# Attention value products: one block per sequence in every second period instead of two half blocks, with eight probability buffers instead of four

## The chip, the cores and the metric

The kernel runs on one NeuronCore of a Trainium2 chip. The metric is the device time of one execution in microseconds (us). Engines are named as the profile names them: PE (TensorE, matmuls), PEld (its weight loads), DVE (VectorE), ACT (ScalarE), POOL (GpSimd), SP (the queue that issues most DMAs).

## What is computed

A decoder of two layers over 32 sequences of 128 tokens with 256 channels, all in float32. Each layer is: layer norm, self-attention, residual; layer norm, attention over a context, residual; layer norm, feed-forward, residual. Three of the six parts are multi-head attentions with 16 heads of 16 channels, and the change lies in these three. Cut to what matters:

```python
def mha(xq, xkv):                      # self-attention: xq is xkv
    q, k, v = split_heads(xq @ Wq), split_heads(xkv @ Wk), split_heads(xkv @ Wv)
    scores = einsum('bhqd,bhkd->bhqk', q, k) / sqrt(16)
    probs = softmax(scores)            # over 128 keys
    out = einsum('bhqk,bhkd->bhqd', probs, v)
    return merge_heads(out) @ Wo
```

The first one (stage a0 below) also has rotary position factors on q and k and biases; the third (stage a2) takes k and v from the context and has a key mask and biases.

## The kernel before, in words

The six parts are six stages, one after the other: a0 (self-attention, about 15 to 285 us of the profile), b0, c0, a1 (self-attention, about 680 to 935 us), a2 (masked attention over the context, about 935 to 1240 us), d1. Stages a0, a1 and a2 are three calls of one function, `attention_stage` (line 526).

**Tiling.** A stage works on 16 groups (NG) of two sequences (PAIR). A group has 8 steps (STEPS): steps 0 to 3 belong to its first sequence, steps 4 to 7 to its second, and a step is four heads of one sequence (QH). Per step and engine:

- `scores` (PE, lines 952 and 961) computes the scores twice, in two banks of PSUM: S1 (queries on the rows, one pass) for the row maxima, S2 (keys on the rows, three passes with split high and low parts) for the exponent. It uses row strips of 32: an S matmul contracts over 32 rows only, and the matmuls of two steps alternate. In stage a2 `mask_step` (line 993) adds the mask to S1.
- `max_step` (DVE, line 830) takes the row maxima of S1. In stage a2 a `shift_step` of POOL (line 687) forms mask minus maximum from it.
- `shift_step` (PE, line 1006, or 1003 in stage a2) subtracts the maxima in S2. PE does this one pair of steps after `scores`.
- `exp_step` (ACT, line 723) writes exp of S2 into a buffer of `probs`, one of four. It waits until the value products of the step that used the buffer before are done (`av_full`).
- `av_step` (PE, line 1019) multiplies probabilities by values: four matmuls per step, one per head, each with 32 columns of weights (16 value channels and a column of ones for the denominator), so the four heads lie in four column strips of the array. Output is bank AV[0] for the first sequence, AV[1] for the second. Each of these float32 matmuls is two records in the trace.

After the four steps of a sequence ACT copies its AV bank out (`raw_heads`, line 728), PE turns it (`turn`, line 1026), DVE divides by the denominators (lines 836 and 839), PE turns it back (`turn_back`, line 1032), ACT and DVE split it into high and low parts (lines 733 and 843).

**Order.** Every engine has its own program, and the order in each is written out by hand. For PE it is `group` at the end of the function: four periods per group, t = 0, 2, 4, 6, each handling two steps. A period of PE is, in this order: `scores` of steps t and t+1 (and the three passes of steps t-2 and t-1), in a2 the mask, `shift_step` of t-2 and t-1, `turn` (t = 0 and 4) or `turn_back` (t = 2 and 6), then one piece of projection work: at t = 0 `output` of an earlier group and `transposes` of the next group's normalised input (line 188), at t = 2 `queries` of the next group, at t = 4 its `keys`, at t = 6 its `values` (all on line 104). The period ends with `av_step` of steps t-4 and t-3, 8 matmuls. Steps with a negative number belong to the group before.

**Waits around it.** PE executes in program order. `scores` of a period waits for the row maxima of the steps before (`max_ok`) and for the exps of the pair whose S2 banks it writes again (`exp_ok`). `queries` waits for the low part of the transposed input, which DVE makes (line 198) from what ACT has copied (line 194) from the output of `transposes`. In stage a2, POOL's program at t = 4 is: shift of step 4, the layer norm's reciprocal root of a later group (`pool_rstd`, lines 172 and 174), shift of step 5; PE needs both shifts at t = 6.

Of the kernel before, what the change touches and what calls it, by code (L numbers as in the profile page):

```python
# [18 lines left out]
ACT = mybir.ActivationFunctionType  # L19
AXX = mybir.AxisListType.X  # L20

P = 128
# [6 lines left out]
H, DH = 16, 16  # L29
QH = 4  # L30
HV = 2
NQ = H // QH
STEPS = PAIR * NQ
# [11 lines left out]
def at_least(eng, sem, value):  # L45

    if not isinstance(value, int) or value > 0:
        eng.wait_ge(sem, value)
# [19 lines left out]
class Names:  # L68
# [7 lines left out]
    def sb(self, name, shape, dt=FP32):  # L76
        return self.ctx.enter_context(self.nc.sbuf_tensor(f"{self.stage}_{name}", shape, dt))
# [4 lines left out]
    def sem(self, name):  # L82
        handle = self.sem_ctx.enter_context(self.nc.semaphore(f"{self.stage}_{name}"))
        self.sems.append(handle)
        return handle
# [440 lines left out]
def attention_stage(nc, name, before, norm, next_norm, consts, wt, following, spare, context=None, next_context=None, mask_dram=None,  # L526
# [3 lines left out]
    sb, sem = nm.sb, nm.sem  # L530
    ident, ident_b, neg_ident_b, head_mask = (consts[k] for k in ("ident", "ident_b", "neg_ident_b", "head_mask"))

    probs = sb("probs", [P, 4, QH * P])
    if x_dram is not None:
        wt.stage(nm, probs[:, 0:KC, :])
    following.stage(nm)
# [23 lines left out]
    S2 = [nm.ps(f"S2_{i}") for i in range(2)]  # L560
# [26 lines left out]
    s1_full, max_ok, s2_full, exp_ok, av_full = (sem(n) for n in ("s1_full", "max_ok", "s2_full", "exp_ok", "av_full"))  # L587
# [22 lines left out]
    def has_window(G):  # L610
        return not isinstance(G, int) or G + 1 < NG
# [9 lines left out]
    def has_step(G, t):  # L621

        return not isinstance(G, int) or 0 <= STEPS * G + t < STEPS * NG

    def whole(G):
        return not isinstance(G, int) or 0 <= G < NG

    def place(t, parity):

        tt = t % STEPS  # L630
        return tt // NQ, tt % NQ, (1 - parity if t < 0 else parity)
# [13 lines left out]
    with nc.Block() as block:  # L645
# [70 lines left out]
        def _(act):  # L716
            if x_dram is None:
                wt.wait_in(act)
            def exp_step(G, t, parity):
                T = G * STEPS + t  # L720
                act.wait_ge(s2_full, T + 1)
                at_least(act, av_full, T - 3)
                act.activation(probs[:, t % 4, :], S2[t % 2][:], ACT.Exp, scale=DH ** -0.5).then_inc(exp_ok, 1)  # L723

            def raw_heads(B, b):
                act.wait_ge(av_full, B * NQ + NQ)
# [219 lines left out]
        def _(pe):  # L946
# [18 lines left out]
            def scores(G, t, parity):  # L965

                T = G * STEPS + t
                first, second = has_step(G, t), has_step(G, t - 2)
                if cross and isinstance(G, int) and G == 0 and t == 0:
                    pe.wait_ge(setup, 1)  # L970
                if first:
                    if t == 0:
                        pe.wait_ge(qmhi_ok, HV * (G + 1))
                        pe.wait_ge(khi_ok, G + 1)
                    at_least(pe, max_ok, T)
                if second:
                    if t == 2:
                        pe.wait_ge(qmlo_ok, HV * (G + 1))
                        pe.wait_ge(klo_ok, G + 1)
                    at_least(pe, exp_ok, T - 2)  # L980
                for i in range(3 * KC):
                    if second:
                        for u in range(2):
                            s2_pass(t - 2 + u, parity, i // 3, i % 3)
                    if first and i < KC * HV:
                        for u in range(2):
                            last = s1_head(t + u, parity, i // HV, i % HV)
                            if i == KC * HV - 1 and not cross:
                                last.then_inc(s1_full, 1)

            def mask_step(G, t):

                pe.matmul(S1[t % 2][:], ident_b[:], add_mask[:].rearrange("p h k -> p (h k)"), start=False, stop=True,  # L993
                          skip_group_check=True).then_inc(s1_full, 1)
# [15 lines left out]
            def av_step(G, t, parity):  # L1010
                T = G * STEPS + t
                b, j, par = place(t, parity)
                if t == 0:
                    pe.wait_ge(v_free, G + 1)
                if t % NQ == 0:
                    at_least(pe, olo_ok, G * PAIR + t // NQ - 1)
                pe.wait_ge(exp_ok, T + 1)
                for h in range(QH):
                    last = pe.matmul(AV[b][32 * h:32 * h + 32, j * P:(j + 1) * P], v_pad[par][:, b, j * QH + h, :],  # L1019
                                     probs[:, t % 4, h * P:(h + 1) * P], start=True, stop=True)  # L1020
                last.then_inc(av_full, 1)

            def turn(B, b):
                pe.wait_ge(raw_ok, B + 1)
                for r in range(NQ):
                    last = pe.transpose(AV[b][:, r * P:(r + 1) * P], av_raw[:, r * P:(r + 1) * P], ident[:])
                last.then_inc(turned, 1)
# [93 lines left out]
            def group(G, parity):  # L1121
                for t in range(0, STEPS, 2):
                    if vo_bias and t == 0 and isinstance(G, int) and G == 0:
                        pe.wait_ge(vo_added, PAIR)
                    scores(G, t, parity)
                    if cross and has_step(G, t):
                        mask_step(G, t)
                        mask_step(G, t + 1)
                    if has_step(G, t - 2):
                        shift_step(G, t - 2)  # L1130
                        shift_step(G, t - 1)
                    if t in (0, 4) and whole(G - 1):
                        turn((G - 1) * PAIR + t // 4, t // 4)
                    if t in (2, 6) and whole(G - 1):
                        turn_back((G - 1) * PAIR + t // 4, t // 4)
                    if t == 0 and whole(G - 2):
                        output(G - 2)
                    if t == 0:
                        transposes(G)
                    if t == 2 and has_window(G):  # L1140
                        queries(G, parity)
                    if t == 4 and has_window(G):
                        keys(G)
                    if t == 6 and has_window(G):
                        values(G)
                    if vo_bias and t == 6 and isinstance(G, int) and G < 0:
                        value_bias()
                    if t == 6 and isinstance(G, int) and G == NG:
                        output(G - 1)
                    if has_step(G, t - 4):  # L1150
                        av_step(G, t - 4, parity)
                        av_step(G, t - 3, parity)
                    if isinstance(G, int) and G >= NG - 1:
                        for u in range(2):
                            following.pe_slot(pe, (G - NG + 1) * STEPS + t + u, NEXT_BANKS,
                                              ((next_norm.lo_ok, 1), (max_ok, NG * STEPS)))
# [819 lines left out]
```

## Time and profile before

| what | us |
|---|---|
| median of 3 runs (lowest, highest) | 1435.04 (1432.97, 1438.40) |
| the profiled execution's own time | 1437.27 |
| its span, first to last instruction | 1435.5 |
| PE busy in the span | 1344.6 (94%) |
| PEld busy | 1195.7 (83%) |
| DVE busy | 1002.7 (70%) |
| ACT busy | 781.9 (54%) |
| POOL busy | 371.4 (26%) |

Matmuls are pipelined: one record lasts some 0.27 us although the next starts 0.11 us after it, so times of PE are read from start to start. A row of the timeline gives the start (us from the span's start), the time to the end of the last record that it merges, the engine, the line, the operation, output <- inputs, partitions x elements, the number of records merged, and in brackets the idle time before it with the work that ended it. The order of the rows is that of their starts.

### The profile page before, as it was taken

To read this page: it belongs to the slowest core of one execution; us is meant where nothing else is said; L and a number is where in the kernel's file an instruction comes from. 1 tells how busy PE (TensorE), PEld (TensorE's weight loads), DVE (VectorE), ACT (ScalarE), POOL (GpSimd) and SP (SyncE) were. 2 spreads that over 40 slices of the span, in tenths; PEclk is the share of its full clock that TensorE was granted. 3 is DMA by queue.
4 is the path that set the end of the run, shared out by engine and by line. 5 is a ranking of instruction groups with operands and counts; after the bars stand their busy time and mean duration, and the time that the engine had idled before them with its cause. 6 is when DMAs were issued, how large, how long until landed. Compare 5 with 4: busy or idle time off the path is not lost. (4 is left out here: it accounts for less than half of the span.)

```text
span 1435.5 us, 41753 instructions
## 1 busy us (share of the span) xinstructions
PE 1344.6 (94%) x15796; PEld 1195.7 (83%) x15796; DVE 1002.7 (70%) x2423; ACT 781.9 (54%) x1569; POOL 371.4 (26%) x458
## 2 busy tenths in 40 slices
PE   5999999899978999998999999889999999689887
PEld 5888888789968999998888888778888888578777
DVE  5888888555555545454777777677777777688885
ACT  2555555345554445453655555545555556377786
POOL 1212212011011212110000000055555555134442
PEclk9999999999998999999999999999999999899999
DMA  6000000031000000001000000020000000000000
GB/s 226 3 2 0 0 0 2 2 117 37 29 21 10 1 0 0 0 1 44 10 3 0 0 0 1 2 78 20 17 15 15 15 8 2 1 16 22 29 23 30
DMA packets 16478, 28.74 MB, mean 20 GB/s; under 512 B 3616, under 2 KB 7712, under 8 KB 16000
## 3 DMA queue, kind: packets, MB, share of 16 engines
q1 hardware_dynamic: 16384, 27.44, 5.8%
q8 instruction: 64, 1.05, 0.3%
q14 instruction: 30, 0.25, 0.1%
HBM read 23.24 MB, written 4.19 MB: 19 GB/s over the span
## 5 line engine op out<-in xcount | busy, mean ns | idle before, releaser
L723 ACT ACTIVATE a_probs<-a_S 128x512 f32<-128x512 f32 x384 | 208.5, 594 | 155.3 <-PE a_S L1006 85.9
L830 DVE TENSOR_REDUCE a_row_max<-a_S 128x4 bf16<-128x512 f32 (+1 forms) x384 | 247.1, 685 | 54.9 <-PE a_S L993 33.1
L172 POOL TENSOR_TENSOR all_var_eps<-all_moments,all_ln_eps 128x2 f32<-128x2 f32 x96 | 25.0, 261 | 727.9 <-DVE all_moments L167 727.9
L961 PE MATMUL a_S<-a_qm_hi,all_odd_split 32*128 32x256 f32 x1536 | 188.7, 303 | 7.6 <-DVE a_row_max L830 3.6
L961 PEld LDWEIGHTS a_S<-a_qm_hi,all_odd_split 32*128 32x128 f32 x1536 | 132.0, 184 | 46.8 <-issue 39.0
L687 POOL TENSOR_TENSOR a_shifts<-a_add_mask,a_row_max 128x512 bf16<-128x512 bf16 x128 | 131.0, 1039 | 119.4 <-DVE a_row_max L830 119.4
L952 PE MATMUL a_S<-all_odd_split,a_qm_hi 32*128 32x128 f32 x1536 | 127.8, 284 | 1.7 <-DVE all_odd_weights L938 1.7
L1019 PE MATMUL a_AV<-a_probs,a_v_pad 128*32 128x128 f32 x3072 | 123.7, 279 | 0.0
L180 DVE TENSOR_SCALAR all_xn<-all_x_res,all_moments,all_rstd 128x256 f32 (+1 forms) x192 | 99.6, 560 | 19.6 <-POOL all_rstd L174 18.8
L961 PE MATMUL a_S<-a_qm_lo,all_odd_split 32*128 32x256 f32 x768 | 108.9, 277 | 0.0
L952 PEld LDWEIGHTS a_S<-all_odd_split,a_qm_hi 32*128 32x128 f32 x1536 | 100.6, 186 | 2.7 <-DVE all_odd_weights L938 2.5
L104 PE MATMUL c_OUT<-all_odd_split,c_h_hi 128*128 128x256 f32 x512 | 94.8, 283 | 0.9 <-DVE all_x_res L1574 0.9
L1019 PEld LDWEIGHTS a_AV<-a_probs,a_v_pad 128*32 128x32 f32 x3072 | 72.2, 109 | 27.5 <-issue 9.8
L843 DVE TENSOR_TENSOR all_odd_split<-a_AV,all_odd_split 128x256 fp32r<-128x256 f32 x96 | 40.8, 425 | 66.1 <-ACT all_odd_split L733 66.1
L104 PE MATMUL a_FA<-all_odd_split 128*128 128x256 f32 x576 | 84.2, 298 | 2.8 <-DVE all_odd_split L843 2.8
L1726 ACT ACTIVATE d_y<-d_ZT,all_even_weights 128x256 f32<-128x256 f32 x128 | 65.0, 559 | 33.4 <-PE d_ZT L1803 33.4
L104 PEld LDWEIGHTS c_OUT<-all_odd_split,c_h_hi 128*128 128x128 f32 x512 | 80.9, 192 | 1.0 <-issue 1.0
L728 ACT ACTIVATE a_av_raw<-a_AV 128x512 f32<-128x512 f32 x96 | 57.8, 602 | 42.9 <-PE a_AV L1019 42.7
L1503 ACT ACTIVATE c_h<-c_HB,all_odd_weights 128x256 f32<-128x256 f32 x128 | 53.8, 472 | 49.6 <-PE c_HB L1613 48.7
L1006 PE MATMUL a_S<-all_neg_ident_b,a_row_max 128*128 128x128 bf16 x1024 | 79.8, 221 | 0.0
L104 PEld LDWEIGHTS a_FA<-all_odd_split 128*128 128x128 f32 x576 | 75.2, 199 | 3.7 <-DVE all_odd_split L843 3.4
L174 POOL TENSOR_TENSOR all_rstd<-all_var_eps,all_minus_half 128x2 f32<-128x2 f32 x96 | 73.6, 767 | 7.5
(250 smaller groups left out, 3869.5 us busy)
## 6 DMA issues: line engine op xcount, KB each, us to landing
all_cx<-in_ctx SPq DMA_DIRECT2D x32, 256.0 KB, 2.7
all_x_res<-in_x SPq DMA_DIRECT2D x8, 512.0 KB, 8.0
out_x<-all_x_res SPq DMA_DIRECT2D x16, 256.0 KB, 2.0
b_routed_wi<-in_L_ffn_wi_W SPq DMA_DIRECT2D x1, 1024.0 KB, 5.2
b_routed_wo<-in_L_ffn_wo_W SPq DMA_DIRECT2D x1, 1024.0 KB, 7.1
all_even_weights<-in_L_ffn_W_fc SPq DMA_DIRECT2D x1, 1024.0 KB, 5.3
all_even_weights<-in_L_ffn_W_proj SPq DMA_DIRECT2D x1, 1024.0 KB, 7.0
a_a_raw<-in_L_attn_Wqkv SPq DMA_DIRECT2D x1, 512.0 KB, 4.0
```

The costliest lines, as they stand in the source:

```text
L104: last = pe.matmul(out, w(k), m(k), start=(k == 0 and n == 0), stop=(k == chunks - 1 and n == 2))
L174: pool.tensor_tensor(self.rstd[:], self.var_eps[:], self.minus_half[:], ALU.pow).then_inc(self.rstd_ok, 1)
L180: last = dve.tensor_scalar(self.xn[:, b, :], self.x(w, b), self.moments[:, b, 0:1], self.rstd[:, b:b + 1], ALU.subtract, ALU.mult)
L687: pool.tensor_tensor(shifts[:, t % 4], add_mask[:], row_max[:, t % 4, :].rearrange("p (h o) -> p h o", o=1).to_broadcast([P, QH, P]), ALU. ...
L723: act.activation(probs[:, t % 4, :], S2[t % 2][:], ACT.Exp, scale=DH ** -0.5).then_inc(exp_ok, 1)
L728: act.activation(av_raw[:], AV[b][:], ACT.Copy).then_inc(raw_ok, 1)
L830: dve.tensor_reduce(row_max[:, t % 4, :], S1[t % 2][:].rearrange("p (h k) -> p h k", h=QH), AXX, ALU.max).then_inc(max_ok, 1)
L952: return pe.matmul(S1[t % 2][:, at * P:(at + 1) * P], qm_hi[parity][strip, c, b, v, :], k_hi[parity][strip, c, tok], start=(not cross or a ...
L961: pe.matmul(S2[t % 2][:, c * HV * P:(c + 1) * HV * P], k[par][strip, c, tok], q[par][strip, c, b].rearrange("p h t -> p (h t)"), start=(c ...
L1006: last = pe.matmul(part, row_max[:, t % 4, h:h + 1].to_broadcast([P, P]), neg_ident_b[:], start=False, stop=h == QH - 1, skip_group_check= ...
L1019: last = pe.matmul(AV[b][32 * h:32 * h + 32, j * P:(j + 1) * P], v_pad[par][:, b, j * QH + h, :], probs[:, t % 4, h * P:(h + 1) * P], star ...
L1726: last = act.activation(y32[n][:, m * TOK:(m + 1) * TOK], ZT[n][:, m * TOK:(m + 1) * TOK], ACT.Identity, bias=offset[:, f:f + 1], scale=ga ...
```

## The change

It alters three things in `attention_stage`: `probs` has 8 buffers (STEPS) instead of 4, so that a step's number in the group is its buffer; `exp_step` waits for the value products of eight steps before instead of four; and PE no longer does two steps of value products at the end of each period, but four steps, all of one sequence, at the end of the periods t = 2 (steps 4 to 7 of the group before) and t = 6 (steps 0 to 3 of this group). The periods t = 0 and t = 4 have none.

```diff
-    probs = sb("probs", [P, 4, QH * P])
+    probs = sb("probs", [P, STEPS, QH * P])
...
-                at_least(act, av_full, T - 3)
-                act.activation(probs[:, t % 4, :], S2[t % 2][:], ACT.Exp, scale=DH ** -0.5).then_inc(exp_ok, 1)
+                at_least(act, av_full, T - STEPS + 1)
+                act.activation(probs[:, t % STEPS, :], S2[t % 2][:], ACT.Exp, scale=DH ** -0.5).then_inc(exp_ok, 1)
...
                 for h in range(QH):
                     last = pe.matmul(AV[b][32 * h:32 * h + 32, j * P:(j + 1) * P], v_pad[par][:, b, j * QH + h, :],
-                                     probs[:, t % 4, h * P:(h + 1) * P], start=True, stop=True)
+                                     probs[:, t % STEPS, h * P:(h + 1) * P], start=True, stop=True)
...
-                    if has_step(G, t - 4):
-                        av_step(G, t - 4, parity)
-                        av_step(G, t - 3, parity)
+                    if t in (2, 6) and has_step(G, t - 6):
+                        for u in range(NQ):
+                            av_step(G, t - 6 + u, parity)
```

The order of PE's instructions in stage a0, group 1, at the end of its period t = 4 (`keys` into bank FB, then the scores of the next period):

```order
 L104 MATMUL a_FB<-all_xT_hi,all_odd_split 128x256 x2
 L104 MATMUL a_FB<-all_xT_lo,all_odd_split 128x256
-L1019 MATMUL a_AV<-a_probs,a_v_pad 32x128 x8
 L961 MATMUL a_S_0<-a_qm_hi,all_odd_split 128x256
 L961 MATMUL a_S_1<-a_qm_hi,all_odd_split 128x256
```

The block of 8 value products is gone, and the scores follow the keys directly. The same holds at the end of t = 0, where the transposes stand ahead of it.

The order of PE at the end of the period t = 6 of the same group (`values` into bank FA, then the scores of the next group):

```order
 L104 MATMUL a_FA<-all_odd_split,all_xT_lo 128x256
 L104 MATMUL a_FA<-all_odd_split,all_xT_hi 128x256
-L1019 MATMUL a_AV<-a_probs,a_v_pad 32x128 x8
+L1019 MATMUL a_AV<-a_probs,a_v_pad 32x128 x16
 L961 MATMUL a_S_0<-a_qm_hi,all_odd_split 128x256
 L961 MATMUL a_S_1<-a_qm_hi,all_odd_split 128x256
```

The block has grown to 16. The same holds at the end of t = 2, behind the queries. The orders of DVE and of POOL are unchanged.

The order of ACT in the loop of stage a0, with the semaphores waited for (`exp_step` between its other work):

```order
 L739 ACTIVATE a_qm_hi<-a_q,all_head_mask 128x4x128
 L721 REGISTER_ALU
-L723 ACTIVATE a_probs<-a_S_0 128x512 [waits a0_av_full,a0_s2_full]
-L721 REGISTER_ALU
-L723 ACTIVATE a_probs<-a_S_1 128x512 [waits a0_av_full,a0_s2_full]
+L48 REGISTER_ALU [waits a0_s2_full]
+L723 ACTIVATE a_probs<-a_S_0 128x512 [waits a0_av_full]
+L721 REGISTER_ALU
+L48 REGISTER_ALU [waits a0_s2_full]
+L723 ACTIVATE a_probs<-a_S_1 128x512 [waits a0_av_full]
```

The exps stay where they were; the value waited for needs one more register instruction ahead of each, which now carries the wait for the scores.

## Rows read from the trace of the kernel before

**Rows 1.** Page, part 1: busy us (share of the span) and instructions

```profile
PE 1344.6 (94%) x15796; PEld 1195.7 (83%) x15796; DVE 1002.7 (70%) x2423; ACT 781.9 (54%) x1569; POOL 371.4 (26%) x458
```

**Rows 2.** Windows over the steady parts of a0, a1, a2: length, then busy us

```profile
core 0: us, PE busy (x) PEld busy (x) DVE busy (x) ACT busy (x) POOL busy (x), PEclk, DMA share, GB/s
57.00:275.00 218.00, 216.93 (x3336) 189.65 (x3332) 181.52 (x391) 119.12 (x234) 42.05 (x52) 1.00 0.00 1
700.00:925.00 225.00, 222.94 (x3443) 194.44 (x3442) 173.51 (x370) 129.95 (x248) 12.17 (x27) 1.00 0.00 1
960.00:1215.00 255.00, 254.28 (x3626) 213.01 (x3625) 194.13 (x427) 142.29 (x275) 151.24 (x158) 1.00 0.05 13
```

**Rows 3.** Page, part 5: the value products, all stages

```profile
L1019 PE MATMUL a_AV<-a_probs,a_v_pad 128*32 128x128 f32 x3072 | 123.7, 279 | 0.0
```

**Rows 4.** Timeline of PE, a1 group 0: queries to scores directly, then keys, block, scores

```profile
685.43 0.28 PE L104 MATMUL a_FA<-all_xT_lo,all_even_split 128*128 128x256 f32 x1
685.64 0.39 PE L961 MATMUL a_S<-a_qm_hi,all_odd_split 32*128 32x256 f32 x2
...
688.36 0.28 PE L104 MATMUL a_FB<-all_xT_lo,all_even_split 128*128 128x256 f32 x1
688.57 0.64 PE L1019 MATMUL a_AV<-a_probs,a_v_pad 128*32 128x128 f32 x16
689.14 0.39 PE L961 MATMUL a_S<-a_qm_hi,all_odd_split 32*128 32x256 f32 x2
```

**Rows 5.** Windows of 0.01 us inside that block: (x) is its records in flight

```profile
688.56:688.57 0.01, 0.00 (x1) 1.00 0.00 0
688.69:688.70 0.01, 0.01 (x4) 1.00 0.00 0
688.72:688.73 0.01, 0.01 (x8) 1.00 0.00 0
688.80:688.81 0.01, 0.01 (x8) 1.00 0.00 0
688.83:688.84 0.01, 0.01 (x12) 1.00 0.00 0
688.91:688.92 0.01, 0.01 (x8) 1.00 0.00 0
688.94:688.95 0.01, 0.01 (x12) 1.00 0.00 0
```

**Rows 6.** Timeline of a1: transposes at t = 0, their split, queries at t = 2

```profile
804.30 0.60 PE L188 MATMUL a_FB<-all_ident,all_xn 128*128 128x128 f32 x4
804.93 0.60 ACT L194 ACTIVATE all_xT_hi<-a_FB 128x512 fp32r<-128x512 f32 x1 [1.36 <-PE a_FB L188]
805.57 0.69 DVE L198 TENSOR_TENSOR all_xT_lo<-a_FB,all_xT_hi 128x512 fp32r<-128x512 f32 x1 [0.26 <-ACT all_xT_hi L194]
806.89 0.30 PEld L104 LDWEIGHTS a_FA<-all_xT_hi,all_even_split 128*128 128x128 f32 x2
```

**Rows 7.** Timeline of a0: the last exps of a group against the next scores

```profile
207.36 1.07 ACT L723 ACTIVATE a_probs<-a_S 128x512 f32<-128x512 f32 x2
208.68 0.39 PE L961 MATMUL a_S<-a_qm_hi,all_odd_split 32*128 32x256 f32 x2
```

**Rows 8.** Timeline of a2, periods t = 4 and 6: mask, maxima, POOL, shift products

```profile
1112.73 0.60 PE L993 MATMUL a_S<-a_add_mask,all_ident_b 128*128 128x512 bf16 x2
1113.40 1.29 DVE L830 TENSOR_REDUCE a_row_max<-a_S 128x4 f32<-128x512 f32 x2
1114.18 1.04 POOL L687 TENSOR_TENSOR a_shifts<-a_add_mask,a_row_max 128x512 bf16<-128x512 bf16 x1 [2.54 <-DVE a_row_max L830]
1115.45 1.16 POOL L174 TENSOR_TENSOR all_rstd<-all_var_eps,all_minus_half 128x2 f32<-128x2 f32 x1
1116.58 1.03 POOL L687 TENSOR_TENSOR a_shifts<-a_add_mask,a_row_max 128x512 bf16<-128x512 bf16 x1
1117.07 0.60 PE L993 MATMUL a_S<-a_add_mask,all_ident_b 128*128 128x512 bf16 x2
1117.50 1.29 DVE L830 TENSOR_REDUCE a_row_max<-a_S 128x4 f32<-128x512 f32 x2 [0.79 <-PE a_S L993]
1117.52 0.61 PE L1003 MATMUL a_S<-all_ident_b,a_shifts 128*128 128x128 bf16 x8
```

**Rows 9.** Timeline of a2, group 0: PE waits for POOL between two shift products

```profile
958.91 0.40 PE L1003 MATMUL a_S<-all_ident_b,a_shifts 128*128 128x128 bf16 x4 [0.92 <-POOL a_shifts L687]
```

**Rows 10.** Timeline of PE and ACT at the end of stage a1

```profile
918.50 0.39 PE L961 MATMUL a_S<-a_qm_hi,all_odd_split 32*128 32x256 f32 x2 [0.98 <-DVE a_row_max L830]
...
928.07 0.64 PE L1019 MATMUL a_AV<-a_probs,a_v_pad 128*32 128x128 f32 x16
928.78 0.60 ACT L728 ACTIVATE a_av_raw<-a_AV 128x512 f32<-128x512 f32 x1 [0.22 <-PE a_AV L1019]
```

## The prediction

> **What bounds the kernel now.** I read the page first: PE is busy 94% of the span [rows 1]. That is an average over six stages, so I took the steady part of each attention stage by itself: PE is busy 216.93 of 218 us in a0, 222.94 of 225 in a1 and 254.28 of 255 in a2, at a granted clock of 1.00, while DVE, the next, has 181.52, 173.51 and 194.13 [rows 2]. So in these stages PE's own stream sets the time: what shortens it counts fully, as long as no other engine becomes late. Then I read the timeline around the value products, from start to start, to see what a block of them costs on PE, and last, for each wait that PE passes, how long before PE's arrival the work was done.
>
> **What a block costs.** The change computes nothing less: 3072 records of value products in 192 blocks of 16 records [rows 3] become 96 blocks of 32. What can be saved is what a block costs beside its own streaming. Group 0 of a1 shows the pair side by side. Without a block, the last projection matmul and the first scores matmul start 0.21 us apart (685.43, 685.64). With one, the block starts 0.21 us behind the projection, and the scores 0.57 us behind the block (688.57, 689.14) [rows 4]. So a block of 8 matmuls costs 0.57 us. Inside it the records start in waves of four, one per column strip: 688.565, then near 688.70, 688.81 and 688.92, that is 0.135, 0.11 and 0.11 us apart, and the exit from the last wave to the scores is 0.22 us, 0.11 more than one more wave would take [rows 5, 4]. Eight more matmuls in a block that is already running are four more waves, 4 x 0.11 = 0.44 us. **Each removed block therefore saves 0.57 - 0.44 = 0.13 to 0.135 us**: one exit (0.11) and a slow first wave (0.025). The bounds: nothing, if every further step in a long block costs what it costs in a block of its own; 0.17 us, if a wave takes 0.10 us, which windows of 0.01 us leave open. I take 0.135, since three of the four intervals are direct readings.
>
> The Trainium skill, "TensorEngine Tiling (Array Packing)", Key Properties, says that changing the tiling mode, and not merely the tile, drains the engine. The trace agrees that a change of shape costs time: 0.21 us from projection to scores against 0.11 between like matmuls. By the rule alone a removed block would save one such change, 0.10 us, 8.9 us for 89 blocks where the rows give 12.0.
>
> **How many.** Each attention stage loses 32 blocks, 96 in all. They count only where PE is the bound. At the end of a1 and a2 the engine waits for row maxima that DVE, busy with the next stage's weights, delivers late (0.98 us in one case) [rows 10]; there the three blocks of the last group and the drain save nothing. I give a0 31, a1 29 and a2 29: 89 x 0.135 = **-12.0 us**.
>
> **What PE meets earlier.** In a group the period ends t = 0 and t = 4 come 0.57 us sooner, and t = 2 and t = 6 come 0.44 later. Behind each there is a wait.
>
> - t = 0 to t = 2, **queries** wait for the split of the transposes: they end at 804.90, ACT copies until 805.53, DVE is done at 806.26, and PE loads the first weights at 806.89 [rows 6]. That is 0.63 us of slack, of which 0.57 goes. A release takes 0.03 to 0.04 us in these rows (804.90 to 804.93, 805.53 to 805.57); I take 0.05 for PE. It just fits: 0 to 0.1 us per group, and I take 0. In a2 the mask and the context transposes add time ahead of it.
> - t = 6 to t = 0, **scores** wait for the exps of steps 4 and 5: done at 208.43, needed at 208.68 [rows 7]. These exps hang on a chain through DVE that starts at the queries of t = 2; between that and the scores PE's stream becomes longer (+0.44 - 0.57 + 0.44 = +0.31), so the slack grows. The extra register instruction ahead of each exp lies on ACT, which is busy 119 of 218 us [rows 2], and inside this slack. Cost 0; without the slack it would be a few hundredths of a us per exp.
> - t = 4 to t = 6 in **a2**, the shift products wait for POOL. POOL starts the shift of step 4 0.78 us behind the start of the maxima, then the reciprocal root (1.16 us), then the shift of step 5, done at 1117.61, which is 3.43 us after POOL's start. PE's products with it are the fifth to eighth of the eight records that start at 1117.52, 0.056 us apart, so they start at 1117.74 [rows 8]: a slack of 0.13 us less 0.05 for the release. With the change PE is there 0.44 - 0.57 = 0.13 us sooner, counted from the queries, at 1117.61. And POOL is later: the maxima of step 4 start at 1113.40 because DVE was busy until then, although the mask product started at 1112.73; the mask product of the new order starts 0.44 us later, at 1113.17, and maxima start 0.43 us behind it (1117.07, 1117.50) [rows 8], at 1113.60. So POOL ends 0.20 us later, at 1117.81, and PE goes on at 1117.86: **a new wait of 0.25 us**, in the 15 groups that have the reciprocal root, **+3.75 us**. Behind it on PE stand the turn back, the values and all that follows, so it counts. That this wait is real can be seen in group 0, where PE already stands 0.92 us for POOL at this place [rows 9]. Its bounds are 0 (POOL just in time) and 0.92 us.
>
> **The eight buffers** take away nothing that was waited for: no exp waits for value products in the rows of the steady parts. The bank AV is freed by work of t = 3 and t = 7, and its first write only comes later than before.
>
> **Ends of the stages.** In the drain, ACT copies the bank as soon as the last value product is done [rows 10]; that block now has 16 matmuls, +0.44 us, and PE has 0.57 us less ahead of it, some of it then spent in waiting. Between -0.4 and +1.3 us for three stages; I take +0.4.
>
> **Sum:** -12.0 + 3.75 + 0.4 = -7.85 us. Against the profiled execution, 1437.27, that is 1429.4; against the median of the runs, 1435.04, which is 2.2 us lower, it is **1427.2 us**. A measurement of this kernel can tell about 0.5%, 7.2 us, from no change; the forecast is just past that, at 0.55%.
>
> **Rivals.**
>
> 1. *POOL stays in time in a2*, and all 89 blocks count: -12.0 + 0.4 gives 1423.4. For it: spans of POOL are rough, and its end leads PE's need by only hundredths. Against: both the delayed maxima and the earlier PE point the same way. Chance 0.2.
> 2. *The saving is eaten almost everywhere*: the queries of a0 and a1 wait 0.1 us (30 groups, 3 us), and a wave in a long block takes 0.12 (89 x 0.04 = 3.6 us), which leaves -7.85 + 6.6 = -1.3, 1433.8. For it: 0.63 us of slack against 0.62 needed. Against: no row of a stall there. Chance 0.22.
> 3. *Slower*: POOL's wait has the size of group 0, 0.92 us in 15 groups of a2, 13.8 us instead of 3.75, with the drain at its bad end (+1.3): -12.0 + 13.8 + 1.3 = +3.1, 1438.1. With the drain as I took it, the change loses from (12.0 - 0.4) / 15 = 0.77 us per such group on. For it: the place is the same; against: in group 0 POOL started later for reasons of the start. To be slower by more than 0.5% a wait of (12.0 + 7.2) / 48 = 0.40 us would have to appear in every group of all three stages. Chance 0.08, 0.05 of it past 0.5%.
>
> My forecast itself has a chance of 0.5. It is so near the bound of 0.5% that I count 0.3 of it as faster and 0.2 as within. **Faster by over 0.5%:** 0.3 + 0.19 of rival 1 = 0.49. **Within 0.5%:** 0.2 + 0.01 + 0.22 + 0.03 = 0.46. **Slower:** 0.05. The range goes from rival 1 less 1 us for a shorter wave (1422.5) to rival 2 (1434).
>
> **What the profile would show.** Blocks of 32 records that take 1.01 us from their start to the scores' (0.97 to 1.05 fits); 0.21 us from projection or transposes to scores at the ends of t = 0 and t = 4. A group of a0 and of a1 shorter by 0.27 us, a group of a2 by 0.02 (the period of two groups of a0 by 0.54 us). In a2 a stall of about 0.25 us between the fourth and the fifth product on line 1003, put down to POOL, fifteen times, and no stall of PE on line 104 in a0 and a1. The forecast is wrong if the block takes over 1.1 us, if groups of a2 shrink as those of a1 do, or if the scores wait for exps or maxima in the steady part.

## The result, and the profile after

| | before | changed |
|---|---|---|
| median of 6 runs (lowest, highest), us | 1436.62 (1432.97, 1438.64) | 1423.38 (1420.69, 1427.06) |
| the profiled execution's own time | 1437.27 | 1422.83 |
| its span | 1435.5 | 1420.9 |

The ratio is 0.9912, with an interval of 0.9897 to 0.9927: the changed kernel is faster by 0.9%, which is more than the 0.5% that a measurement can tell. The time lies inside the range that was given. The gain, 13.2 us by the medians, is larger than the forecast 7.85. The same kernel timed again beside other runs of before gave 1426.26 against 1435.66, 0.9936 (0.9923 to 0.9949), 9.4 us. Between such comparisons the median of one kernel moves by up to 3 us, so I count on a gain of 9 to 13 us.

The page of the changed kernel, part 1, with busy us, share of the span and instructions, against [rows 1]; and the row of the value products from part 5, against [rows 3]:

```profile
PE 1329.2 (94%) x15796; PEld 1197.8 (84%) x15796; DVE 1001.7 (70%) x2423; ACT 782.4 (55%) x1569; POOL 371.4 (26%) x458
...
L1019 PE MATMUL a_AV<-a_probs,a_v_pad 128*32 128x128 f32 x3072 | 103.8, 276 | 0.0
```

Nothing less is computed: 15796 matmul records and 3072 of value products, as before. PE's busy time fell by 15.4 us, about as much as the span. The value products' busy time counts each stretch in which at least one record is in flight, and it fell from 123.7 to 103.8 although a record takes as long as before (276 ns, 279 before): the tail of a block, in which its last records are still in flight, is there 96 times and no longer 192.

**The block.** Timeline of PE in the changed kernel, a1 group 0, where [rows 4] are from: keys directly followed by scores, then values, block, scores.

```profile
682.50 0.28 PE L104 MATMUL a_FB<-all_xT_lo,all_even_split 128*128 128x256 f32 x1
682.71 0.38 PE L961 MATMUL a_S<-a_qm_hi,all_odd_split 32*128 32x256 f32 x2
...
685.44 0.28 PE L104 MATMUL a_FA<-all_even_split,all_xT_hi 128*128 128x256 f32 x1
685.65 1.08 PE L1019 MATMUL a_AV<-a_probs,a_v_pad 128*32 128x128 f32 x32
686.66 0.38 PE L961 MATMUL a_S<-a_qm_hi,all_odd_split 32*128 32x256 f32 x2
```

The block of 32 records takes 1.01 us from its start to the scores' (685.65, 686.66), and keys to scores 0.21 us (682.50, 682.71), both as forecast. The second half of a block is indeed 0.44 us, not 0.57.

**The groups.** A period of a group is read from one block of transposes (line 188) to the next. Timeline of PE in before, stage a0, then in the changed kernel:

```profile
196.43 0.60 PE L188 MATMUL a_FB<-all_ident,all_xn 128*128 128x128 f32 x4
...
211.93 0.60 PE L188 MATMUL a_FB<-all_ident,all_xn 128*128 128x128 f32 x4
227.49 0.60 PE L188 MATMUL a_FB<-all_ident,all_xn 128*128 128x128 f32 x4
```

```profile
192.28 0.60 PE L188 MATMUL a_FB<-all_ident,all_xn 128*128 128x128 f32 x4
...
207.50 0.60 PE L188 MATMUL a_FB<-all_ident,all_xn 128*128 128x128 f32 x4
222.72 0.60 PE L188 MATMUL a_FB<-all_ident,all_xn 128*128 128x128 f32 x4
```

| period of a group, us | before | in before, at the end of a loop pass | changed | at the end of a loop pass |
|---|---|---|---|---|
| a0 | 15.50 | 15.75 | 15.22 | 15.24 to 15.29 |
| a1 | 15.62 | 15.84 to 15.87 | 15.34 | 15.38 to 15.42 |
| a2 | 17.74 | 17.95 to 18.06 | 17.74 | 17.77 to 17.81 |

The groups of a0 and a1 are shorter by 0.28 (forecast 0.27), those of a2 by nothing (forecast 0.02). But in before every second group inside the loop was some 0.23 us longer, and in the changed kernel it hardly is. The loop has five passes and so four branches back, and each stage has four such groups; behind the fifth pass, where PE goes straight on, there is none. That column I had not seen.

**The wait in a2.** Timeline of the changed kernel, the periods t = 4 and 6, where [rows 8] are from:

```profile
1101.19 0.60 PE L993 MATMUL a_S<-a_add_mask,all_ident_b 128*128 128x512 bf16 x2
1101.62 1.29 DVE L830 TENSOR_REDUCE a_row_max<-a_S 128x4 f32<-128x512 f32 x2
1102.39 1.04 POOL L687 TENSOR_TENSOR a_shifts<-a_add_mask,a_row_max 128x512 bf16<-128x512 bf16 x1 [2.73 <-DVE a_row_max L830]
1103.66 1.16 POOL L174 TENSOR_TENSOR all_rstd<-all_var_eps,all_minus_half 128x2 f32<-128x2 f32 x1
1104.79 1.03 POOL L687 TENSOR_TENSOR a_shifts<-a_add_mask,a_row_max 128x512 bf16<-128x512 bf16 x1
1105.40 0.88 PE L1003 MATMUL a_S<-all_ident_b,a_shifts 128*128 128x128 bf16 x8
1105.88 0.23 PEld L1003 LDWEIGHTS a_S<-all_ident_b,a_shifts 128*128 128x128 bf16 x4 [0.27 <-POOL a_shifts L687]
```

The mask product is 0.43 us ahead of the maxima, POOL ends at 1105.82, and the fifth shift product is loaded at 1105.88. The eight products take 0.88 us instead of 0.61: a wait of 0.27 us where 0.25 was forecast. It doesn't stand on PE's row, since the matmuls are pipelined; the row of the weight load has it, in each of the groups 1 to 14. In group 0 the wait of [rows 9], which PE's row does show, grew from 0.92 to 1.24 us.

**Where the 14.6 us of the two spans lie:** from the transposes in group 1 to the last ones in group 15, 14 periods, a0 gives 4.66 us, a1 4.35 and a2 0.58, together 9.6. The other 5.0 us lie outside these stretches: 0.67 ahead of a0's, 0.67 from a0's to a1's, 0.62 from a1's to a2's, and 3.05 behind a2's. So three readings needed tests: the block and the wait, the loop's end, and what lies outside the stretches.

### The profile page after: what moved, and what is told of

The parts are those of the page before. It is cut to its first block and busy times, and to the rows that moved or that the text cites. A ratio compares the mean times of both kernels' runs of the same rounds, so it can differ in the third digit from the quotient of the medians.

```text
span 1420.9 us, 41741 instructions
## 1 busy us (share of the span) xinstructions
PE 1329.2 (94%) x15796; PEld 1197.8 (84%) x15796; DVE 1001.7 (70%) x2423; ACT 782.4 (55%) x1569; POOL 371.4 (26%) x458
## 5 line engine op out<-in xcount | busy, mean ns | idle before, releaser
L1019 PE MATMUL a_AV<-a_probs,a_v_pad 128*32 128x128 f32 x3072 | 103.8, 276 | 0.0
L1019 PEld LDWEIGHTS a_AV<-a_probs,a_v_pad 128*32 128x32 f32 x3072 | 78.0, 109 | 13.0 <-issue 1.5
```

## Experiments

The theory: a removed block gives 0.14 us, a2 gives most of it back to POOL, and the ends of loop passes give what I had overlooked. The rivals: the buffers or the exps do it (an earlier exp frees the S2 banks); or a wait of PE's other than the loop's was removed.

**1. The buffers alone.** The first three hunks of the change, PE's order as before.

```diff
-    probs = sb("probs", [P, 4, QH * P])
+    probs = sb("probs", [P, STEPS, QH * P])
...
-                at_least(act, av_full, T - 3)
+                at_least(act, av_full, T - STEPS + 1)
```

> Eight probability buffers and the looser wait of the exps, with the value products still in two steps per period. My theory: the buffers free nothing that was waited for, so the time is that of the kernel before, within 1.5 us, and the groups of a0 keep their 15.50 and 15.75 us. Rival (the buffers themselves bring a part of the 13 us measured): 3 us or more faster.

Measured: 1434.88 beside 1436.02 of before, ratio 0.999 (0.998 to 1.0), and every period of the table as in before. Eight buffers by themselves give nothing that can be told from no change.

**2 and 3. One merge at a time.** Eight buffers; in the first kernel only the first sequence's products are done together (t = 6), in the second only the second's (t = 2).

```diff
-                    if has_step(G, t - 4):
+                    if t == 6 and has_step(G, 0):
+                        for u in range(NQ):
+                            av_step(G, u, parity)
+                    if t in (0, 2) and has_step(G, t - 4):
                         av_step(G, t - 4, parity)
                         av_step(G, t - 3, parity)
```

```diff
-                    if has_step(G, t - 4):
+                    if t == 2 and has_step(G, -4):
+                        for u in range(NQ):
+                            av_step(G, u - 4, parity)
+                    if t in (4, 6) and has_step(G, t - 4):
                         av_step(G, t - 4, parity)
                         av_step(G, t - 3, parity)
```

> Eight buffers; only the first sequence of a group is merged: a block of 16 at the end of t = 6, none at t = 4, blocks of 8 at t = 0 and t = 2 as before. Block theory: 46 counting blocks x 0.135 = 6.2 us faster. Loop theory (the 0.22 us stall at the loop's end, 15 times, goes where the block ahead of the branch has 16 matmuls): 3.3 us more. POOL theory: PE reaches the shift products of a2 0.57 us earlier against a slack of 0.08, so it waits 0.49 us in 15 groups: 7.4 us back. Sum: about 2 us faster than before, a group of a2 0.36 us longer than the 17.74 of before. Without the POOL theory: 9.5 us faster.

> Eight buffers; only the second sequence is merged: a block of 16 at the end of t = 2, none at t = 0, blocks of 8 at t = 4 and t = 6. Block theory: 6.2 us faster. Loop theory: the block ahead of the branch is still one of 8, so the 0.22 us stall stays. POOL theory: PE reaches the shift products later, no wait, a group of a2 is 17.60 us. Sum: 6 us faster than before. If the loop's stall goes here too, 9.5 us.

Measured: the merge at t = 6 gives 1436.12, ratio 1.0001 (0.9991 to 1.0012), nothing where some 2 us were expected; the merge at t = 2 gives 1428.66, 0.9954 (0.9941 to 0.9967), 7.4 us where 6 were. The periods tell why. With t = 6 merged, a group of a0 takes 15.40 (15.48 at the loop's end) and of a1 15.48, so 0.10 to 0.14 less each, and the long groups at the loop's end are gone but for 0.03 to 0.09 us; but a group of a2 takes 18.00 outside the loop and 18.11 to 18.15 in it, 0.26 to 0.41 more than 17.74. Timeline of this kernel in a2:

```profile
1113.70 1.16 POOL L174 TENSOR_TENSOR all_rstd<-all_var_eps,all_minus_half 128x2 f32<-128x2 f32 x1
...
1115.19 0.39 PE L1003 MATMUL a_S<-all_ident_b,a_shifts 128*128 128x128 bf16 x4
...
1115.92 0.23 PEld L1003 LDWEIGHTS a_S<-all_ident_b,a_shifts 128*128 128x128 bf16 x4 [0.52 <-POOL a_shifts L687]
1115.92 0.40 PE L1003 MATMUL a_S<-all_ident_b,a_shifts 128*128 128x128 bf16 x4 [0.35 <-POOL a_shifts L687]
```

The wait for POOL is 0.52 us here: the period t = 4 has lost its whole block, so PE is 0.57 us sooner, and nothing was added ahead of it at t = 2. First and fifth product are 0.73 us apart where 0.22 would do ([rows 8]: eight products start 0.056 us apart), and this 0.51 less the 0.14 of a removed block is the 0.37 by which the groups in the loop are longer. Outside the loop PE's row shows a wait of 0.23 instead of 0.35, and the group is 0.26 longer. With t = 2 merged, POOL isn't waited for (the block at t = 4 is still there), a2 takes 17.60, 0.14 less, a0 15.36, 0.14 less, and the long groups stay (15.6 in a0, 15.69 in a1, 17.83 in a2). So a removed block is worth 0.14 us in each stage, the wait comes from t = 4, and what happens at the loop's end comes from the block at t = 6.

**4 and 5. Without the loop.** The 16 groups of a stage written out instead of a loop of two groups, for before and for the changed kernel.

```diff
-        for G in range(-1, 3):
-            group(G, G % 2)
-        with eng.Fori(1, (NG - 4) // 2) as i:
-            group(i * 2 + 1, 1)
-            group(i * 2 + 2, 0)
-        for G in range(NG - 3, NG + 1):
+        for G in range(-1, NG + 1):
             group(G, G % 2)
```

> The kernel before with all groups of the attention stages written out, no loop on any engine. Loop theory: 15 stalls of 0.22 us go, 3.3 us faster, all groups of a0 take 15.50 us. Rival (the longer groups have another cause, such as the parity of the group): no change and alternating groups.

> The changed kernel with no loop in the attention stages. Loop theory: the stall at the loop's end is already gone, so within 1 us of the changed kernel, 13 us faster than before. Against the unrolled kernel before it shows the blocks and the POOL wait alone: 8 to 10 us.

Measured: before without the loop 1433.77, ratio 0.9987 (0.9976 to 0.9997), 2.25 us less (2.8 by the rows of the three stretches), and the groups that ended a pass lose their extra 0.2 us (15.50 in a0 with some of 15.56, 15.62, 17.74). The changed kernel without the loop takes 1422.3, 0.9912 (0.9896 to 0.9929), and its profiled execution has the periods that it has outside the loop; the three stretches are 0.7 us shorter. So before lost 2.8 us at the loop's end, and the changed kernel loses 0.7. The lines in before, at the end of a pass in a2, first PE's timeline, then the weight loads':

```profile
1101.75 0.64 PE L1019 MATMUL a_AV<-a_probs,a_v_pad 128*32 128x128 f32 x16
1102.55 0.39 PE L961 MATMUL a_S<-a_qm_hi,all_odd_split 32*128 32x256 f32 x2 [0.15 <-issue]
```

```profile
1102.54 0.19 PEld L961 LDWEIGHTS a_S<-a_qm_hi,all_odd_split 32*128 32x128 f32 x2 [0.42 <-issue]
```

The block takes 0.80 us to the scores, not the 0.57 of [rows 4], and no engine is named as the one waited for: "issue". PE's branch back to the loop's start stands between the two. The same place in the changed kernel:

```profile
1090.09 1.08 PE L1019 MATMUL a_AV<-a_probs,a_v_pad 128*32 128x128 f32 x32
1091.13 0.39 PE L961 MATMUL a_S<-a_qm_hi,all_odd_split 32*128 32x256 f32 x2
```

```profile
1091.12 0.19 PEld L961 LDWEIGHTS a_S<-a_qm_hi,all_odd_split 32*128 32x128 f32 x2 [0.22 <-issue]
```

That is 1.04 us instead of the 1.01 elsewhere. The weight load still stands, 0.22 us instead of 0.42, but behind a block of 1 us little of it reaches the matmuls: the stall is hidden and not gone. Between the two kernels without a loop the medians differ by 11.5 us, where 8 to 10 were expected (the two stood beside different runs of before), and the spans of their profiles by 11.1. Of it the stretch of a0 gives 4.0, that of a1 3.7 and that of a2 -0.2, 7.5 in all, a little less than 28 x 0.28 = 7.8 because PE waits for an exp in group 1 of each stage of the changed kernel (0.16 us on its row). 3.6 us by the spans are left for what lies outside.

**6 and 7. POOL's reciprocal root after both shifts.** In POOL's program the root moves from t = 4 to t = 5, behind the shift of step 5; once on the changed kernel, once on before.

```diff
-                    if has_norm(G) and t == 4:
+                    if has_norm(G) and t == 5:
                         norm.pool_rstd(pool, G + 2)
-                    if first_of_next(G) and t == 4:
+                    if first_of_next(G) and t == 5:
                         next_norm.pool_rstd(pool, 0)
```

> The changed kernel with POOL's reciprocal root moved behind the shift of step 5 instead of ahead of it. POOL theory: the wait of 0.27 us between the shift products of a2 goes in 15 groups, a group of a2 falls from 17.74 to 17.47 us, 4 us faster than the changed kernel, about 17 us faster than before. Rival (PE is held by something else there, or the normalisation becomes late by the later root): no gain, or up to 1 us per group lost in a wait for the transposes.

> The kernel before with the same move on POOL alone. Theory: the wait did not exist before the change (PE had 0.08 us of slack), so the time is that of the kernel before within 1.5 us. Rival (the wait was there before): up to 4 us faster.

Measured on the changed kernel: 1420.25 against 1435.57, 0.99 (0.9882 to 0.9917), 15.3 us where about 17 were expected. The period of a2 is 17.47 instead of 17.74, 0.27 less, while a0 and a1 stay, and group 0 of a2 is 1.35 us shorter. Timeline of a2:

```profile
1099.04 2.04 POOL L687 TENSOR_TENSOR a_shifts<-a_add_mask,a_row_max 128x512 bf16<-128x512 bf16 x2 [2.73 <-DVE a_row_max L830]
1101.03 0.64 POOL L172 TENSOR_TENSOR all_var_eps<-all_moments,all_ln_eps 128x2 f32<-128x2 f32 x1
1101.76 1.09 POOL L174 TENSOR_TENSOR all_rstd<-all_var_eps,all_minus_half 128x2 f32<-128x2 f32 x1
...
1102.04 0.61 PE L1003 MATMUL a_S<-all_ident_b,a_shifts 128*128 128x128 bf16 x8
```

Both shifts are done 0.96 us before the products, which take 0.61 us again. On before the same edit gives 1433.39, 0.9988 (0.9973 to 1.0002), and leaves the steady periods at 17.74 and 17.95; only group 0, with the wait of [rows 9], is shorter by 1.1 us. So before had no wait in the steady part, the changed kernel has one of 0.27 us per group, and its cause is the root between the two shifts.

**8. The changed order with four buffers.** PE's order of the change, `probs` with four buffers and the old wait.

```diff
-    probs = sb("probs", [P, STEPS, QH * P])
+    probs = sb("probs", [P, 4, QH * P])
...
-                at_least(act, av_full, T - STEPS + 1)
+                at_least(act, av_full, T - 3)
```

> The new order of the value products with the old four buffers and the old wait of the exps. Theory: the exps of steps 4 and 5 (and 0 and 1) can start only when the block has done its first steps, some 0.5 us into it, and take 1.09 us, so the scores behind the block wait about 0.6 us, twice per group, 94 times: 60 us slower than the changed kernel. Rival (the buffers are not needed): as the changed kernel.

Measured: 1524.65, ratio 1.062 (1.0597 to 1.0644), 101 us over the changed kernel where I expected some 60. Periods 17.23, 16.75 and 20.78. Timeline of a0:

```profile
165.37 1.08 PE L1019 MATMUL a_AV<-a_probs,a_v_pad 128*32 128x128 f32 x32
165.86 1.08 ACT L723 ACTIVATE a_probs<-a_S 128x512 f32<-128x512 f32 x2 [2.89 <-PE a_AV L1019]
167.09 0.39 PE L961 MATMUL a_S<-a_qm_hi,all_odd_split 32*128 32x256 f32 x2 [0.64 <-ACT a_probs L723]
170.95 0.39 PE L961 MATMUL a_S<-a_qm_hi,all_odd_split 32*128 32x256 f32 x2 [0.51 <-ACT a_probs L723]
174.05 1.08 PE L1019 MATMUL a_AV<-a_probs,a_v_pad 128*32 128x128 f32 x32
175.74 0.39 PE L961 MATMUL a_S<-a_qm_hi,all_odd_split 32*128 32x256 f32 x2 [0.61 <-ACT a_probs L723]
```

ACT stands 2.89 us for the block, its exps are late, and PE stands for them: block to scores is 1.72 and 1.69 us instead of 1.01. Those two waits, 0.68 to 0.71 us per block, were expected; the third (0.51 us, behind the period without a block) was not: ACT's late exps push back its other work and, through it, DVE's, which feeds ACT again. The three, 0.71, 0.68 and 0.51, are 1.9 of the 2.0 us by which a group of a0 is longer; the 3.0 us in a2 I did not take apart. So the buffers give nothing by themselves, and without them the new order costs more than it brings.

**9. The blocks cut in two.** In the changed kernel 8 of the 16 matmuls of a block are done ahead of the period's projection, so there are 192 blocks again, in other places.

```diff
+                    if t in (2, 6) and has_step(G, t - 6):
+                        for u in range(2):
+                            av_step(G, t - 6 + u, parity)
                     if t == 2 and has_window(G):
                         queries(G, parity)
...
                     if t in (2, 6) and has_step(G, t - 6):
-                        for u in range(NQ):
+                        for u in range(2, NQ):
```

> The changed kernel with each block of 16 cut in two: 8 value products ahead of the queries (t = 2) or the values (t = 6), 8 behind them. Block theory: every cut adds a change of shape on the way in (0.21 - 0.11 = 0.10 us), a slow first wave (0.025) and an exit (0.11): 0.235 us, 0.47 per group, about 90 times, 21 us slower than the changed kernel. Rival (only the number of changes between value products and scores counts): as the changed kernel.

Measured: 1456.89, ratio 1.0151 (1.0138 to 1.0164), 30.6 us more than the changed kernel beside it (1426.26), where I expected 21. Periods: 15.91 in a0, 16.00 in a1, 18.36 to 18.41 in a2, so 0.62 to 0.69 more per group, and 0.22 more at the loop's end, since the block ahead of the branch is short again. Timeline of a0, period t = 2:

```profile
209.94 0.39 PE L1032 MATMUL a_AV<-all_ident,a_o_tok 128*128 128x128 f32 x2
210.25 0.64 PE L1019 MATMUL a_AV<-a_probs,a_v_pad 128*32 128x128 f32 x16
210.83 0.39 PE L104 MATMUL a_FA<-all_odd_split,all_xT_hi 128*128 128x256 f32 x1
211.05 0.28 PE L104 MATMUL a_FA<-all_odd_split,all_xT_lo 128*128 128x256 f32 x1
...
212.44 0.65 PE L1019 MATMUL a_AV<-a_probs,a_v_pad 128*32 128x128 f32 x16
213.01 0.39 PE L961 MATMUL a_S<-a_qm_hi,all_odd_split 32*128 32x256 f32 x2
```

A block costs more here than between projection and scores. Turn back to projection takes 0.15 us without a block between them and 0.89 with it (209.94 to 210.83), and the projection itself starts as slowly with the block as without (0.22 us between its first two matmuls here, 0.20 in a1 of the changed kernel, at 684.05, where no block stands ahead). The second block takes 0.57. A cut thus costs 0.89 - 0.15 + 0.57 - 1.01 = 0.30 us in these rows and 0.31 to 0.35 by the periods: that a block costs something beside its streaming is shown a second time, and that the amount depends on its neighbours too.

**10. The products ahead of the values.** At t = 6 the whole block stands ahead of `values` instead of behind them.

```diff
+                    if t == 6 and has_step(G, 0):
+                        for u in range(NQ):
+                            av_step(G, u, parity)
                     if t == 6 and has_window(G):
                         values(G)
...
-                    if t in (2, 6) and has_step(G, t - 6):
+                    if t == 2 and has_step(G, t - 6):
```

> The changed kernel with the block of t = 6 ahead of the values, so that the values stand between it and the scores. One more change of shape per group, 0.10 us: 4.6 us slower than the changed kernel. It also tests what goes ahead of the loop's branch: 24 records of projection that run for 1.5 us instead of 64 of value products that run for 1.0. If the stall at the loop's end is hidden by running time ahead of the branch, it stays away; if it needs the long block there, it comes back as 0.2 us or more in every second group, 3 us more.

Measured: 1434.67, ratio 0.9991 (0.9979 to 1.0002), 8.4 us more than the changed kernel beside it, where I expected 4.6. A group takes 0.23 us more in a0 (15.45), 0.22 in a1, 0.19 in a2. Timeline of a0, period t = 6:

```profile
219.18 0.39 PE L1032 MATMUL a_AV<-all_ident,a_o_tok 128*128 128x128 f32 x2
219.49 1.08 PE L1019 MATMUL a_AV<-a_probs,a_v_pad 128*32 128x128 f32 x32
```

Into the block PE needs 0.31 us instead of the 0.21 behind a projection; the change of shape between values and scores (0.21) stays as well. So one more change of shape costs 0.2 us, twice what I took. And the long groups at the loop's end don't come back, although what runs ahead of the branch is now projection work, about 1.5 us of it: it isn't the kind of work that hides the branch. Some 1.0 us of value products and 1.5 us of projection hide it, 0.57 us of value products doesn't. But it isn't simply PE's running time either: in before these 0.57 us stand behind 1.5 us of projection that PE runs without a break. What about the last piece of work decides, no run shows.

**11 and 12. The changed kernel again, and the best version.** The second takes the edits of 6 (POOL's root late) and 5 (no loop) together.

> The changed kernel once more, as the base for the three others of this call: 1423 us.

> The changed kernel with POOL's reciprocal root behind the shift of step 5 and without loops. From the runs so far: 15.22, 15.34 and 17.47 us per group, 3 to 4 us faster than the changed kernel for the root and up to 1 us more for the loops: 1419.

Measured: the changed kernel as told above, 1426.26 where 1423 was expected. The combination 1416.49 where 1419 was, ratio 0.9876 (0.9859 to 0.9894), with periods of 15.22, 15.34 and 17.47: faster than before and than the changed kernel, by 19 and 9.8 us in the same comparison. By the periods 14 x 0.27 = 3.8 us of it are POOL's wait, 0.7 the loop's end, and 1.35 the wait in group 0; the rest, about 4 us, is scatter outside the stretches (see the ends of the stages below).

## Why the prediction was right, and where its size was wrong

- **What bounds the kernel:** right. PE's stream sets the time; where a group lost 0.28 us of it the span lost it.
- **A removed block saves 0.135 us:** right. The block of 32 records took 1.01 us, and two removed blocks shortened a group by 0.28. Merging one pair alone gave 0.14 in all three stages when nothing stood in its way. The bounds, 0 and 0.17, were wider than needed. The rule of the Trainium skill, "TensorEngine Tiling (Array Packing)", Key Properties, that a change of tiling mode drains the engine, points the right way, and experiments 9 and 10 agree with it; but one change at the 0.10 us of the rows is less than the 0.14 that a block was worth. Rival 2, a longer wave, is out.
- **Queries and exps:** right. The queries' slack of 0.63 us less 0.57 held, and no PE row of the steady parts names ACT or DVE. But the cost of 0 holds in the steady part alone. In the changed kernel the scores wait for exps at the start of each stage (0.16 us in group 1, and once more in a0 and a2, 0.47 and 0.19 us), where before's rows have no such wait, and longer at the end of a0 (0.60 instead of 0.24 and 0.15).
- **POOL in a2, +0.25 us in 15 groups:** right, 0.27 us each. Both halves of the reason held: PE comes sooner and the maxima later. It came in 14 groups and not 15, since group 0 had its wait already; that one grew by 0.32. Moving the root shortened a group of the changed kernel by 0.27 and none of the steady groups of before. Rivals 1 (POOL in time) and 3 (0.92 us) are out as mechanisms, though rival 1's time, 1423.4, is the one measured, for other reasons.
- **The buffers cost and give nothing:** right, 0.999. The extra register instruction ahead of an exp can't be seen: a pair of exps that waits for nothing takes 1.07 us without it and with it.
- **"They count only where PE is the bound", 89 blocks and nothing else:** here the sum was short. It missed the *end of the loop*. My steady windows [rows 2] showed 1.07, 2.06 and 0.72 us in which PE wasn't busy, and I took them for nothing, without asking which rows they were; the block that I timed lay outside the loop. In each window four rows of "issue" give 0.6 to 0.7 us of it, the stall at the branch. The rest of a0's is 0.4 us of waits for exps in its last group; a1's window reaches into the end of the stage, with 1.3 us of waits for row maxima, those of [rows 10] among them, and 0.15 for an exp. The groups show the stall whole: 0.21 to 0.32 us behind each of four branches in three stages, 2.8 us by the rows and 2.25 by the medians of before without a loop, where my expectation had 15 stalls and 3.3 us. The longer block ahead of the branch hides all but 0.7 us, so the change took 2.1 us there too.
- **Ends of the stages, +0.4 us:** wrong in sign, and outside its bounds of -0.4 and +1.3. From a stage's last transposes to the last turn, a0 takes 19.04 us instead of 19.59, and a1 15.19 instead of 15.34. In a2 it is 18.01 against 18.39 in the profile of experiment 1, which has before's order. That is -1.1 us, and other profiles of the two orders with the loop repeat each of the three within 0.02 (before's own in a2 excepted, see below). In a2's last group it can be seen how, in PE's timeline of before and then of the changed kernel:

```profile
1218.02 0.38 PE L961 MATMUL a_S<-a_qm_hi,all_odd_split 32*128 32x256 f32 x2 [1.28 <-ACT a_probs L723]
...
1227.41 2.91 PE L104 MATMUL a_FA<-all_odd_split 128*128 128x256 f32 x12
```

```profile
1205.89 0.38 PE L961 MATMUL a_S<-a_qm_hi,all_odd_split 32*128 32x256 f32 x2 [0.84 <-ACT a_probs L723]
...
1214.84 1.67 PE L104 MATMUL a_FA<-all_odd_split 128*128 128x256 f32 x12
```

PE stands for exps there in both, and the longer block is done inside that wait, which shrinks from 1.28 to 0.84: the 0.44 us of added products cost nothing, while the removed block ahead of them counts whole (from the last transposes, at 1212.87 and 1201.32, to these scores 5.15 us became 4.57). I had it the other way round, the saving lost in the wait. Later waits then take a part of it back (0.48 us for an exp, 0.65 for DVE).

The output behind it took 1.24 us less, but that is the clock and not the change. The granted clock was 0.50, the lower of its two levels, from 1227.40 to 1230.20 in before's profile, and 1.00 during the same work of the changed kernel. With before's order at the full clock (experiment 1) it took the same 1.67:

```profile
1227.43 1.67 PE L104 MATMUL a_FA<-all_odd_split 128*128 128x256 f32 x12
```

So before's own profile has 19.73 us where experiment 1's has 18.39, and 1.3 of the 5.0 us is this slow output. Another 1.3 lies behind a2's last output, in stage d1, where the change alters nothing. That is no effect but scatter: a second profile of the changed kernel (experiment 11) agrees with the first within 0.1 us in its three stretches together, 677.44 and 677.54 us, and differs by 4.1 outside them, 747.5 and 743.4, where before has 748.4.

The sum again, by rows: 7.5 us from the stretches without a loop and 2.1 at the loop's end make the 9.6 that the stretches show, and 1.1 at the ends makes 10.7. Ahead of the stretches a1 wins 0.15 us more from group 0 to group 1, and a2 loses 0.44, where its wait for POOL grew; that leaves 10.4. It lies between the 9.4 and 13.2 us that the two comparisons measured. The difference between these two is no property of the change: the profiles put it outside the stretches, as scatter. The forecast had 12.0 - 3.75 = 8.25 for the blocks less POOL's wait, against the 7.5, then nothing for the loop, and +0.4 instead of -1.1. That the first measurement, 1423.38, lies inside the range owes something to luck: the fast edge of 1422.5 was drawn for rival 1, which did not happen, and what carried the time there was the loop's end, the ends of the stages and scatter.

## What to carry to other kernels

When small blocks of another tile shape are cut into a stream of matmuls, put them together: each block cost 0.14 us beside its work, and 0.30 to 0.35 us between other neighbours. Then ask which engine fed PE behind the block that has gone, and look for low-priority work, such as POOL's root here, that stands between two results that PE needs. Compare the periods of successive groups before trusting one of them, since a stall at a loop's end shows only in every second one and names no engine.

## What the runs showed of the hardware

- PE's branch back at the end of a loop pass cost 0.21 to 0.32 us behind a block of 0.57 us, and little behind 1.0 us of one block (0.02 to 0.08) or 1.5 us of projections (0.01 at most). Behind the 1.0 us block the weight load still stood 0.22 us (0.42 in before). That instructions for the new pass are fetched while the queued ones run would explain it, but no run measured that.
- A change of shape has no single price: 0.21 us from projection to products, and 0.31 from transposing products to value products, against 0.11 between like ones.
- A wait in the middle of pipelined matmuls can be absent from PE's rows: 0.27 us stood on the weight load alone, and in the length of the merged row (0.88 for 0.61).
